# One recommender tower on one core: the Gram product taken sample by sample, each on a quarter of TensorE's columns, and two more tables looked up by one-hot products

## What is computed

```python
e = jnp.stack([tbl_0[ids[:, 0]], ..., tbl_26[ids[:, 26]]], axis=1)      # 512 x 27 x 128
z = einsum('bnd,bmd->bnm', e, e)[:, the pairs i < j]                    # 512 x 351
h = jnp.concatenate([z, dense_ctx], axis=1)                             # 512 x 367
h = jnp.maximum(h @ W_top1 + b_top1, 0.0)                               # 512 x 512
h = jnp.maximum(h @ W_top2 + b_top2, 0.0)                               # 512 x 256
y = h @ W_top3                                                          # 512 x 1
```

## Time and profile before

| | us |
|---|---|
| median of 3 runs (lowest, highest) | 117.65 (117.36, 117.71) |
| the profiled execution | 117.24 |
| its span, first to last instruction | 115.4 |
| TensorE busy | 108.6 (94%) |
| DVE, ACT, GpSimd busy | 83.7, 76.4, 67.8 |

### The profile page before, as it was taken

One profiled execution on the slowest core, in us unless ns is written; L12 is line 12 of the kernel. 1 busy time (PEld: TensorE's weight loads), 2 busy tenths in 40 slices (PEclk: granted clock), 3 DMA queues, 4 the chain that ended last, 5 costly groups with the idle time before them and its releaser, 6 DMA issues.

```text
span 115.4 us, 2207 instructions
## 1 busy us (share of the span) xinstructions
PE 108.6 (94%) x729; PEld 96.9 (84%) x729; DVE 83.7 (73%) x287; ACT 76.4 (66%) x208; POOL 67.8 (59%) x72
## 2 busy tenths in 40 slices
PE   5599999999989999999799999999999989999991
PEld 4377886888768888887699899999999989999891
DVE  4699699996999996998858989542895416962121
ACT  5456997789958989984369977822778127971210
POOL 2777777777777777787777777776776000000000
PEclk9999999999999999999999999999999999999999
DMA  2898774886548769930221222221221100001000
GB/s 62 252 290 214 165 204 83 230 216 155 129 124 173 196 162 298 351 101 23 77 45 45 71 62 58 64 71 50 60 60 45 40 9 3 0 0 21 0 6 1
DMA packets 5661, 12.16 MB, mean 105 GB/s; under 512 B 2251, under 2 KB 2987, under 8 KB 5522
## 3 DMA queue, kind: packets, MB, share of 16 engines
q1 hardware_dynamic: 3580, 7.80, 25.0%
q0 software_dynamic: 2048, 4.20, 14.5%
q10 hardware_dynamic: 22, 0.02, 0.1%
HBM read 11.77 MB, written 0.00 MB: 102 GB/s over the span
## 4 chain that ended last, share of the span: by engine, by line
PE 70%; DVE 13%; DMA 6%; ACT 5%; issue 2%; SPq 2%
PE gram_ps L446 15%; PE acc L423 14%; PE acc L461 10%; PE acc L417 10%; DMA table<-in_tbl 6%; DVE onehot L582 5%; PE tr_ps L390 5%; PE acc L485 5%; DVE pairs L539 4%; PE gram_ps L461 3%; PE acc L446 3%; DVE lo L588 3%; ACT embT L637 2%; PE tr_ps L485 2%; PE tr_ps L446 1%
## 5 line engine op out<-in xcount | busy, mean ns | idle before, releaser
L376 POOL DMA_INDIRECT emb<-in_tbl,ids_sb x64 | 67.0, 1047 | 20.5 <-issue 19.2
L582 DVE TENSOR_SCALAR onehot<-idrel 125x512 fp32r<-125x512 f32 x81 | 29.1, 429 | 2.9 <-ACT idrel L651 2.8
L417 PE MATMUL acc<-onehot,hi 125*128 125x512 f32 x92 | 25.1, 419 | 1.0 <-DVE onehot L582 1.0
L539 DVE COPY pairs<-gram_ps 26x48 f32<-26x48 f32 (+1 forms) x96 | 19.5, 204 | 8.4 <-PE gram_ps L446 7.1
L539 ACT COPY pairs<-gram_ps 26x48 f32<-26x48 f32 (+1 forms) x96 | 18.7, 194 | 8.5 <-PE gram_ps L446 7.4
L423 PE MATMUL acc<-onehot,lo 125*128 125x512 f32 x92 | 23.4, 397 | 0.6 <-DVE lo L588 0.6
L446 PE MATMUL gram_ps<-embT 128*122 128x104 f32 x192 | 22.3, 270 | 1.2 <-ACT embT L637 0.7
L446 PEld LDWEIGHTS gram_ps<-embT 128*122 128x122 f32 x192 | 21.3, 187 | 1.7 <-ACT embT L637 0.9
L417 PEld LDWEIGHTS acc<-onehot,hi 125*128 125x128 f32 x92 | 17.7, 199 | 5.4 <-ACT hi L659 2.1
L423 PEld LDWEIGHTS acc<-onehot,lo 125*128 125x128 f32 x92 | 17.4, 191 | 5.4 <-DVE lo L588 1.8
L637 ACT COPY embT<-acc 128x512 f32<-128x512 f32 (+2 forms) x12 | 12.3, 1041 | 6.8 <-PE acc L423 6.8
(11 more groups left out here) (51 smaller groups left out, 84.2 us busy)
## 6 DMA issues: line engine op xcount, KB each, us to landing
table<-in_tbl SPq DMA_DIRECT2D x8, 480.0 KB
table<-in_tbl SPq DMA_DIRECT2D x2, 600.0 KB
emb<-in_tbl,ids_sb POOLq DMA_INDIRECT x64, 3.5
w_sb<-in_W SPq DMA_DIRECT2D x1, 1024.0 KB
w_sb<-in_W SPq DMA_DIRECT2D x1, 512.0 KB, 8.9
table<-in_tbl SPq DMA_DIRECT2D x2, 240.0 KB
pairs<-pairs SPq DMA_DIRECT2D x16, 15.0 KB
table<-in_tbl SPq DMA_DIRECT2D x8, 20.0 KB
```

Source lines behind the costliest of these rows:

```text
L376: pool.indirect_dma_start(emb[:, t % EMB_RING, gathered_features.index(f), :], None, tables[f], bass.IndirectOffsetOnAxis(ids_sb[:, t, f:f ...
L417: nc.tensor.matmul(acc[:, b, 0:batch], hi[0:ROWS_K, b, c, :], one_hot(k, c), start=(c == 0), stop=False)
L539: last = copy(pairs[QUAD * q:QUAD * q + FEATS - 1, t % 2, a:SLOTS, c0:c0 + UNITG], src.rearrange("r g a -> r a g"))
L582: nc.vector.tensor_scalar(one_hot(k, c), idrel[0:ROWS_K, b, 0:batch], float(c), None, ALU.is_equal).then_inc(onehot_by_dve, 1)
```

## The change

- **Gram** is taken one sample at a time: stationary 26 columns (features 0 to 25), moving 26 columns (features 1 to 26), output in the 32 output partitions of quarter `s` of the array, so four samples in a row go to four quarters of the array's columns. 128 products a tile, 512 in all, where there were 128. A whole tile has one half of `gram_ps`; units, the spare buffer and the zeroed pads are gone.
- **Copies** are one for each destination quarter `q` and sample quarter `s`, 26x6x32 or 26x7x32 numbers: 8 a tile on each of DVE and ACT, where there were 32.
- **Row moves**: SP issues the DMA of quarter `q` as soon as both engines have copied `q`, where it waited for all.
- **Look-ups**: features 9 and 10 (1250 rows each) are looked up too, 13 in all; 14 features are fetched, in groups of 4, 4, 4 and 2 (56 DMAs, 56 transposes). Nine transpose groups stand between look-ups.
- **First look-up**: its `hi` and `lo` chunks alternate by half (4 `hi`, 4 `lo`, 4 `hi`, 4 `lo`) on TensorE, and DVE makes the one-hots and `lo` in that order. The load of the third table waits until the second half of the first has landed. For a table in two parts after the first, ACT makes its last one-hot after the second cast.
- **Before it**: four blank products instead of three at the start (`WARM`), and two more behind the first spreads (`FILL`).
- `STEPS` is rewritten: the Gram products of tiles 0 and 1 directly follow the look-ups.

The diff, cut to its core:

```diff
-LOOKED_UP_TABLES = [4, 6, 3, 7, 8, 5, 11, 12, 15, 20, 21]
+LOOKED_UP_TABLES = [4, 6, 3, 7, 8, 5, 11, 12, 9, 15, 20, 10, 21]
...
-    WARM = 3
+    WARM = 4
+    FILL = 2
...
-        gram_ps = pb("gram_ps", [P, 2, UNITG, P])
+        gram_ps = pb("gram_ps", [P, 2, GROUPS * QUAD])
...
-        AT_LOOKUP = {2: ORDER[0], 3: ORDER[1], 5: ORDER[2], 7: ORDER[3], 8: ORDER[4], 9: ORDER[5]}
+        AT_LOOKUP = {2: ORDER[0], 4: ORDER[1], 5: ORDER[2], 6: ORDER[3], 8: ORDER[4], 9: ORDER[5], 10: ORDER[6], 11: ORDER[7], 12: ORDER[8]}
...
+                if k == EARLY:
+
+                    sp.wait_ge(table_loaded[0], 16 * 2)
...
-                sp.wait_ge(pairs_by_dve, UNITS * (t + 1))
-                sp.wait_ge(pairs_by_act, UNITS * (t + 1))
                 sp.wait_ge(ctx_loaded, 16 * 2 * min(t + 2, TILES))
                 for q in range(QUADS):
+                    sp.wait_ge(pairs_by_dve, QUADS * t + q + 1)
+                    sp.wait_ge(pairs_by_act, QUADS * t + q + 1)
...
+                for part in (parts(k) if k == 0 else [slice(0, CHS[k])]):
+                    for c in range(part.start, part.stop):
+                        high(c)
+                    for c in range(part.start, part.stop):
+                        last = low(c)
                 last.then_inc(looked_up, 1)
...
-                for g in range(UNITG):
-                    p0 = SG * (UNITG * n + g)
-                    last = nc.tensor.matmul(unit_ps(t, n)[0:ROWS, g, 0:WIDTH], vectors[:, QUAD * p0:QUAD * p0 + ROWS],
-                                            embT[:, t, p0:p0 + SG, 1:FEATS], start=True, stop=True)
...
+                if t >= 2:
+
+                    pe.wait_ge(pairs_by_dve, QUADS * (t - 1))
+                    pe.wait_ge(pairs_by_act, QUADS * (t - 1))
+                for g in range(GROUPS):
+                    for s in range(SG):
+                        last = nc.tensor.matmul(gram_ps[QUAD * s:QUAD * s + COLS, t % 2, QUAD * g:QUAD * g + COLS],
+                                                embT[:, t, SG * g + s, 0:FEATS - 1], embT[:, t, SG * g + s, 1:FEATS],
+                                                start=True, stop=True)
                 last.then_inc(gram_done, 1)
...
+            for _ in range(FILL):
+                nc.tensor.matmul(tr_ps[:, 1, 0, :], blank[:, :], blank[:, :], start=True, stop=True)
...
+            for s in quarters:
+                src = gram_ps[QUAD * s:QUAD * s + FEATS - 1, t % 2, :].rearrange("r (g c) -> r c g", c=QUAD)
+                last = copy(pairs[QUAD * q:QUAD * q + FEATS - 1, t % 2, a:SLOTS, GROUPS * s:GROUPS * (s + 1)],
+                            src[:, col:col + QUADS * (SLOTS - 1 - a) + 1:QUADS, :])
...
-            nc.vector.memset(embT[:, :, :, FEATS:QUAD], 0.0).then_inc(pads_zeroed, 1)
```

More of the change, by code:

```diff
@@ L267, in build_tower @@
         LAST = TILES - 1
[L268 to L289, removed]
+        Y_AT = 3 * P
         def h1_ps(t, n):
-            return acc[:, n // 2, P * (n % 2):P * (n % 2 + 1)] if t < LAST else gram_ps[:, n // 2, 4 * (n % 2), :]
+            return acc[:, n // 2, P * (n % 2):P * (n % 2 + 1)] if t < LAST else gram_ps[:, n // 2, batch * (n % 2):batch * (n % 2) + P]
         def h2_ps(t, m):
@@ L406, in look_up, with high @@
                     pe.wait_ge(vectors_out, k - 1)
-                for c in range(CHS[k]):
+                def high(c):
                     for n, part in enumerate(parts(k)):
@@ L416, in look_up, with low @@
                         pe.wait_ge(onehot_by_act, k + 1)
-                    nc.tensor.matmul(acc[:, b, 0:batch], hi[0:ROWS_K, b, c, :], one_hot(k, c),
-                                     start=(c == 0), stop=False)
-                for c in range(CHS[k]):
+                    return nc.tensor.matmul(acc[:, b, 0:batch], hi[0:ROWS_K, b, c, :], one_hot(k, c),
+                                            start=(c == 0), stop=False)
+                def low(c):
                     for n, part in enumerate(parts(k)):
@@ L529, in _, with move_pairs @@
                     y(t)
-        def move_pairs(copy, t, n, s):
-            view = unit_ps(t, n)[QUAD * s:QUAD * s + FEATS - 1, :, :]
-            c0 = (P // SG) * s + UNITG * n
-            for q in range(QUADS):
-                a = FIRST_SLOT[q]
-                col = (FEATS - 1) * s + QUADS * a + q - 2
-                src = view[:, :, col:col + QUADS * (SLOTS - 1 - a) + 1:QUADS]
-                last = copy(pairs[QUAD * q:QUAD * q + FEATS - 1, t % 2, a:SLOTS, c0:c0 + UNITG],
-                            src.rearrange("r g a -> r a g"))
+        def move_pairs(copy, t, q, quarters):
+            a = FIRST_SLOT[q]
+            col = QUADS * a + q - 2
+            for s in quarters:
+                src = gram_ps[QUAD * s:QUAD * s + FEATS - 1, t % 2, :].rearrange("r (g c) -> r c g", c=QUAD)
+                last = copy(pairs[QUAD * q:QUAD * q + FEATS - 1, t % 2, a:SLOTS, GROUPS * s:GROUPS * (s + 1)],
+                            src[:, col:col + QUADS * (SLOTS - 1 - a) + 1:QUADS, :])
             return last
@@ L580, in _ @@
                     dve.wait_ge(looked_up, k - 1)
-                for c in range(DVE_CHS[k]):
-                    nc.vector.tensor_scalar(one_hot(k, c), idrel[0:ROWS_K, b, 0:batch], float(c), None,
-                                            ALU.is_equal).then_inc(onehot_by_dve, 1)
+                made = 0
                 for n, c in enumerate(parts(k)):
+                    upto = min(c.stop, DVE_CHS[k]) if k == 0 else DVE_CHS[k]
+                    for one in range(made, upto):
+                        nc.vector.tensor_scalar(one_hot(k, one), idrel[0:ROWS_K, b, 0:batch], float(one), None,
+                                                ALU.is_equal).then_inc(onehot_by_dve, 1)
+                    made = upto
                     dve.wait_ge(hi_ready, parts_to(k) + n + 1)
@@ L601, in _ @@
                 elif kind == "gram":
-                    if t >= 2 and arg == 0:
+                    if t >= 2:
                         dve.wait_ge(h1_done, H1C * (t - 1))
-                    dve.wait_ge(gram_done, UNITS * t + arg + 1)
-                    for s in (0, 1):
-                        last = move_pairs(nc.vector.tensor_copy, t, arg, s)
-                    last.then_inc(pairs_by_dve, 1)
+                    if t == 0:
+                        dve.wait_ge(pairs_zeroed, 1)
+                    dve.wait_ge(gram_done, t + 1)
+                    for q in range(QUADS):
+                        move_pairs(nc.vector.tensor_copy, t, q, (0, 1)).then_inc(pairs_by_dve, 1)
                 elif kind == "h1":
@@ L681, in _ @@
                 elif kind == "gram":
-                    if t >= 2 and arg == 0:
+                    if t >= 2:
                         act.wait_ge(h1_done, H1C * (t - 1))
-                    act.wait_ge(gram_done, UNITS * t + arg + 1)
-                    for s in (2, 3):
-                        last = move_pairs(nc.scalar.copy, t, arg, s)
-                    last.then_inc(pairs_by_act, 1)
+                    if t == 0:
+                        act.wait_ge(pairs_zeroed, 1)
+                    act.wait_ge(gram_done, t + 1)
+                    for q in range(QUADS):
+                        move_pairs(nc.scalar.copy, t, q, (2, 3)).then_inc(pairs_by_act, 1)
                 elif kind == "h1":
```

65 lines of the change are left out of this document (24 added, 41 removed).

## The result

| | before | changed |
|---|---|---|
| median (lowest, highest), us | 117.68 (117.36, 118.22), 4 runs | 125.44 (125.18, 125.85), 4 runs |
| span of the profiled execution | 115.4 | 123.6 |
| TensorE busy | 108.6 (94%) | 108.7 (88%) |
| mean granted clock | 1.00 | 0.93 |

The changed kernel takes 1.068 times as long, 95% interval 1.064 to 1.073. The forecast was 112.9 us and faster; the range ended at 119. TensorE has the same busy time, and there are 8.2 us more span: TensorE stands idle for longer, and part of its busy time is the same work at a slower clock.

What follows compares the result with a forecast made beforehand. TensorE was taken as the bound, DVE a near second in the look-ups. 9.6 + 0.6 - 0.9 - 13.6 + 1.2 + 0.2 - 0.9 - 0.5 = -4.3 us, from 117.24 to 112.9 us; range 107 to 119.

Steps and rivals of the forecast that it cites:

- Part 2: Gram product on TensorE: 1024 records of 26 columns at 13.3 ns take 13.6 us instead of 27.2, -13.6 us.
- rival B: Gram product: all four array quarters load abreast, 6.6 to 11 ns a record, 107.8 us in all; chance 0.22.
- A: Gram product: neighbours on different quarters overlap by half, 11 to 17.5 ns a record, 110.7 to 116 us; chance 0.50.
- 1024 x p: Gram product on TensorE: 1024 records times the price p of one record, 13.3 ns, give 13.6 us.
- rival F: Stretches of small products: the clock falls to its 1.2 GHz level, 124 us or more; chance 0.04.
- Rival C: Gram product: one record at a time, 26 to 30 ns each, 125 up to 129 us, slower; chance 0.13.
- Part 1: Two more look-ups: +9.6 us on TensorE, +0.6 for waits on DVE, -0.9 for eight transposes fewer.
- Part 3: Copies and row moves: DVE copies take 0.35 and 0.38 us; new waits, +1.2 us at tile 0 and +0.2 for h2T.
- Part 5: First look-up's blanks, alternating halves and held third table: between 0 and 0.9 us gained, taken as -0.5.

Runs made afterwards that it cites:

- the version with 11 look-ups: Two samples to a product on a half of the array, pads zeroed by ACT and DVE, reordered steps, 11 look-ups, 64 fetches: 111.21 us, 0.943 of before.
- quarter-by-quarter kernel: Changed kernel with its two Gram loops exchanged, so a tile's products go out one array quarter after another: 124.25 us, 1.055 of the kernel before.

## Why the prediction was wrong, point by point

- **Part 2, the price of a Gram record: too high, and not the step that failed.** I took 13.3 ns between bounds of 6.6 and 26, on the ground that neighbours overlap by half. It is 8.4 to 8.5 in tiles 2 and 3, in rival B's span: three abreast. (In tiles 0 and 1 it is 10.7 and more within a packet, in part at the half clock; the rest is not explained.) B's 107.8 us did not come (and A's lower end is 111.1 by its own rule, not 110.7, with the wait at tile 0), and the upper bound for one load after another, 26, was measured at 25.8 with shared quarters. That also settles two rules of the Trainium skill for this kernel. Tiles do work in parallel (TensorEngine Tiling, Key Properties; the trace agrees, 8.4 against 25.8 ns). That a load overlaps a product only where row groups differ (TensorE: Matmul & The Clock Gate, Part 3: Packing small matmuls) does not hold for quarters that share all 128 rows.
- **What failed is the step from that price to the time: 1024 x p.** It took for granted that TensorE can be fed at any pace; no term of the sum and no rival stood for the supply of instructions. By the supply, 1024 records are 8 pieces of 3.7 us, some 30 us if they stand alone, whatever the array can do; pieces fetched beforehand and the other work among them brought it to 23.1 us in the three stretches of the four tiles, where I had 13.6. The idle part is 10.0 us; the 13.1 without it are near my 13.6 by luck, quick records in two tiles and slow ones in the others. The trace of before had the counts in its table of queues (6 packets, 0.10 MB for 1458 loads and products and little else), but no stall, since 128 records of 106 ns last 13.6 us.
- **The clock, rival F: mechanism wrong, effect real.** I gave it 0.04 as a consequence of small products. It fell behind idle stretches of 2.4 us, and in the version with 11 look-ups behind waits of 2.1 and 2.2 us that had other causes. The three first layers took 15.25 us against 10.9 in the quarter-by-quarter kernel, 4.3 us more, and transposes and the third layer behind the stretches 1.3 more: 5.7 us in all.
- **Rival C had the right time for the wrong reason.** Its 125 us at p = 26 is what came out. Its own evidence, does not stand: the engine started products 8.4 ns apart. The issue floor of about 25 ns that the Trainium skill gives (TensorE: Matmul & The Clock Gate, Back-to-back issue gap) does not bind across quarters here; within one quarter 25.8 ns was measured, which is also the load.
- **Part 1, look-ups.** They ended at 65.3, 9.7 us later than before; I had 10.6. Undone, they gave 7.8, since then TensorE waits 3.2 us for ACT behind tile 0's products.
- **Part 3, copies and moves.** Copies take 348 and 384 ns on DVE, forecast 0.35 and 0.38. The wait of 1.2 us for tile 0's rows did not come: the stops of tile 1 covered it. The last tile waited for nothing, as forecast.
- **Part 5, the start.** 0.5 was forecast and nothing can be told in the total. In the changed kernel's profile the products stayed 0.43 us apart until 9 us in spite of the blanks. In the profile of the quarter-by-quarter kernel, with the same start, they came 0.23 apart from 7.3 us on and the first look-up ended at 9.8 us, near the 9.6 of the forecast; but the look-ups as a whole ended no earlier (65.9 us against 65.3). Whether the blanks bring the pace forward is not shown.
- **In sum:** 112.9 + 9.5 (Gram stretches) + 5.7 (clock outside them) - 1.2 (the wait) - 0.9 (look-ups) = 126.0, against 125.4.

What stays open is why the three parts of the 3.7 us are as long as they are. The packet itself is under way for 1.0 to 1.4 of them; no run here changes the size of a piece or when it is asked for. Nor did a run keep TensorE busy during a stop, and the clock does not fall behind each one: two of 2.3 us in other profiles (the old start, the changed kernel with 11 look-ups) had the full clock behind them.

The Trainium skill (Runtime: NRT & Kernel Launch, Instruction fetch mechanics) says that instructions come in blocks of 16 KiB, 256 instructions, and that crossing a block is mostly hidden. The first half agrees with 16.4 KB a packet. The second nearly holds here at 26 ns a record, with stops of 0.3 and 0.4 us, and not at 8.4, with stops of up to 2.6.

## To carry to other kernels

Count instructions before splitting work into smaller ones: in these runs TensorE got 128 load-and-product pairs every 3.7 us or so, about 29 ns a pair, so making a pair cheaper than that gains nothing in a long row of them, and the idle stretches mostly cost the clock behind them as well. Choose the tile of the array so that a pair lasts about as long as its supply (here two samples on a half, 27 ns), or space short bursts with as much slower work. A bound from the array's side alone is only half a bound.

## What the runs showed that I had not expected

- Products on four different column quarters start 8.4 ns apart though each loads 26 columns of its own; on one quarter 25.8 ns. On halves of the array with 58 columns: 27 ns.
- 128 records (0.20 MB / 12 packets, 16.4 KB) arrive every 3.45 to 4.1 us in a row: 1.1 to 1.4 us until the next packet starts, 0.9 to 1.4 for the packet, 1.3 to 1.5 until TensorE goes on.
- In the changed kernel each of the three idle stretches of 2.35 to 2.6 us on TensorE was followed by 6 to 8 us with a granted clock of 0.53 to 0.72 in the mean; in two other profiles a stop of 2.3 us was not.
- GpSimd's memset of 128x2560 (2.71 us) held DVE's one-hots up for 3.1 us, and for 3.3 in a second kernel.
